# Sixteen batches of a scan, an FP4 network and linear attention on one core: every step's place in the engines' orders set anew

## The reference

```python
x = x + scan(layernorm(x))        # state-space scan, 16 states
x = x + ffn(layernorm(x))         # gate, up, down with FP4 blocks of 16
x = x + attention(layernorm(x))   # causal linear attention, 16 heads
x = x + ffn(layernorm(x))         # the same weights again

# scan
x_in = x @ w_in
dt_low, B, C = split(x_in @ w_x)                 # 64, 16, 16 columns
dt = softplus(dt_low @ w_dt + b_dt) * (DT_MAX - DT_MIN) + DT_MIN
A = -exp(A_log)
h = exp(dt * A) * h + sum_d(dt * A * B * u)      # step by step over 512 rows
y = sum_n(h * C) + Dp * u
# ffn: q() rounds blocks of 16 to FP4 with a scale of its own
y = q(silu(q(x) @ q(w_gate)) * (q(x) @ q(w_up))) @ q(w_down)
# attention: elu + 1 on q and k, sums over all rows so far
num = q_t @ sum(k v);  den = q_t @ sum(k);  y = (num / den) @ W_proj + b_proj
```

## Time and profile before

| | us |
|---|---|
| runs shown: lowest, median, highest of 3 | 2395.42, 2399.52, 3922.05 |
| profiled execution | 2388.81 |
| its span | 2387.1 |
| mean granted TensorE clock | 0.956 |

### The profile page before, as it was taken

The page is one execution under the profiler, slowest core; times in us unless marked ns, Lnnn a source line. Parts: engine busy times, 40 slices in busy tenths (PEclk is TensorE's granted clock), DMA queues, the critical chain, the costliest instruction groups (busy, mean ns, idle before and its releaser), DMA issues. The chain is left out here.

```text
span 2387.1 us, 40867 instructions
## 1 busy us (share of the span) xinstructions
PE 2074.3 (87%) x12844; PEld 1296.4 (54%) x12844; DVE 2055.3 (86%) x3876; ACT 1893.9 (79%) x3800; POOL 1210.0 (51%) x1804
## 2 busy tenths in 40 slices
PE   2448898998989899898989989898998989889887
PEld 1115556464655646465565646556564656646574
DVE  7988998979889897989989798998979899897734
ACT  5779887897978789797878979787897978867453
POOL 7114454545545454554546455454645555464744
PEclk8669899999999999999999999999999999999999
DMA  3542422323132232313223232322223132221000
GB/s 84 134 113 54 107 56 66 83 60 92 47 105 56 70 79 63 89 47 104 56 71 79 65 87 50 102 56 75 75 66 85 52 100 56 70 70 34 5 6 12
DMA packets 104452, 165.98 MB, mean 70 GB/s; under 512 B 15459, under 2 KB 34095, under 8 KB 104239
## 3 DMA queue, kind: packets, MB, share of 16 engines
q1 hardware_dynamic: 104238, 163.37, 25.7%
HBM read 146.55 MB, written 16.78 MB: 68 GB/s over the span
## 5 line engine op out<-in xcount | busy, mean ns | idle before, releaser
L1399 DVE TENSOR_TENSOR_SCAN scan_bufs<-scan_bufs,inp_bank 128x512 f32<-128x512 f32 x512 | 617.8, 1207 | 4.9 <-ACT scan_bufs L794 4.4
L1108 PE MATMUL bank<-w_gu,f_xqT 128*128 128x512 f32 x1024 | 496.6, 630 | 36.3 <-ACT f_xqT L857 35.1
L787 ACT ACTIVATE scan_bufs<-scan_bufs,a_rows 128x512 f32<-128x512 f32 x512 | 371.5, 725 | 54.8 <-DMA scan_bufs<-dt_copy 54.5
L1123 PE MATMUL bank<-w_dn,f_hqT 128*128 128x256 f32 x1536 | 357.9, 383 | 8.6 <-ACT f_hqT L857 8.6
L1108 PEld LDWEIGHTS bank<-w_gu,f_xqT 128*128 128x128 f32 x1024 | 201.1, 202 | 269.1 <-issue 265.0
L1409 DVE TENSOR_TENSOR scan_bufs<-scan_bufs,c_bank 128x512 f32<-128x512 f32 x512 | 343.1, 670 | 1.2
L794 ACT ACTIVATE scan_bufs<-scan_bufs 128x512 f32<-128x512 f32 x512 | 323.6, 632 | 3.9
L1123 PEld LDWEIGHTS bank<-w_dn,f_hqT 128*128 128x128 f32 x1536 | 284.3, 190 | 77.3 <-issue 26.0
L688 POOL TENSOR_TENSOR f_h<-f_h,f_h_scale 128x704 f32<-128x704 f32 x128 | 178.1, 1391 | 283.8 <-DVE f_h L1274 283.8
L710 POOL TENSOR_SCALAR_AFFINE_SELECT masked_scores<-masked_scores 128x512 f32<-128x512 f32 x256 | 168.8, 685 | 217.1 <-ACT masked_scores L857 216.8
L699 POOL TENSOR_TENSOR f_h<-f_h,f_h_lean 128x704 f32<-128x704 f32 x128 | 216.1, 1688 | 122.2 <-DVE f_h L1460 113.1
(11 more groups left out here) (196 smaller groups left out, 4408.3 us busy)
## 6 DMA issues: line engine op xcount, KB each, us to landing
scan_bufs<-dt_copy SPq DMA_DIRECT2D x512, 256.0 KB, 4.1
xp<-L_attn_a_x SPq DMA_DIRECT2D x16, 512.0 KB, 4.1
dt_copy<-dt SPq DMA_DIRECT2D x32, 256.0 KB, 2.8
out<-x SPq DMA_DIRECT2D x64, 128.0 KB, 3.5
w_attn<-L_attn_b_W_attn SPq DMA_DIRECT2D x1, 768.0 KB, 4.9
masked_scores<-L_ffn_w_gate SPq DMA_DIRECT2D x1, 704.0 KB
masked_scores<-L_ffn_w_up SPq DMA_DIRECT2D x1, 704.0 KB
f_h<-L_ffn_w_down SPq DMA_DIRECT2D x2, 352.0 KB, 11.1
```

The lines of the kernel that those rows point to most:

```text
L787: nc.scalar.activation(half, half, ACT.Exp, scale=a_rows[:, c, at:at + 1]).then_inc(root_ready, 1)
L1108: last = nc.tensor.matmul(to[:, :], f.xqT[:, k, :], w_gu[:, k, g, lo:hi], start=(k == 0), stop=(k == DH - 1))
L1123: last = nc.tensor.matmul(to[:, 0:D], f.hqT[:, k, :], w_dn[:, k, :], start=(k == 0), stop=(k == FK - 1))
L1399: nc.vector.tensor_tensor_scan(half, half, inp[:, :], 0.0, ALU.mult, ALU.add)\
```

## The change

All numbers that place steps are replaced. HEAD is written out step by step and its unit is one beat (`HEAD_BEAT` was 0.6), TIMES has new values, LAST_AT and LAST_SHIFT become GAPS and SHIFT. One wait is added: `inp` now names that ACT has copied `B` out of its bank. No instruction that computes is added or removed, but ACT loads its function table 65 times in place of 63, as `log` and `inv` of the two halves of batch 0 now alternate.

```diff
-HEAD_BEAT = 0.6
+HEAD_BEAT = 1.0
 HEAD = {
-    "dve": [(8.0, "P", 0, "stats"), (9.0, "P", 0, "aggr"), (10.0, "W", 0, "tables"),
+    "dve": [
+        (-132.873, "P", 0, "stats"), (-63.924, "P", 0, "aggr"), (-96.677, "W", 0, "tables"),
...
-LAST_AT = {"R1": (66, 3), "R2": (94.7, 4)}
-LAST_SHIFT = {
+GAPS = {(15, 'R2'): -3.0}
+SHIFT = {
+    15: {
...
 TIMES = {
-        ("Y", "finish"): -0.561, ("R1", "a_qkv"): 17.259, ("R2", "down"): 13.035, ("P", "stats"): 3.643,
+        ("Y", "finish"): -0.815, ("R1", "a_qkv"): 17.501, ("R2", "down"): 13.085, ("P", "stats"): 3.232,
...
 def beat_of(engine, part, step, t, b):
-    at = start_of(engine, part, step, t)
-    if b == NB - 1 and part in LAST_AT:
-        first, gap = LAST_AT[part]
-        at += first - PARTS_AT[part][0] + t * (gap - PARTS_AT[part][1])
-        at += LAST_SHIFT.get(engine, {}).get((part, step), 0.0)
+    at = start_of(engine, part, step, t) + t * GAPS.get((b, part), 0.0)
+    at += SHIFT.get(b, {}).get(engine, {}).get((part, step), 0.0)
     return round(BEATS * b + at, 6)
...
                     src, done = wait_filled(dve, "P", b, 0, "G")
+                    wait_drained(dve, "P", b, 0, "B")
```

More of the change, by code:

```diff
@@ L38 @@
 TURNS = PIECES + 4
-HEAD_BEAT = 0.6
-def pieces(step, first, gap, which):
-    return [(first + gap * n, "W", i, step) for n, i in enumerate(which)]
+HEAD_BEAT = 1.0
 HEAD = {
-    "sp": [(-40.0, "P", 0, "load"), (1.6, "P", 0, "keep0"), (8.6, "P", 0, "keep1")],
-    "dve": [(8.0, "P", 0, "stats"), (9.0, "P", 0, "aggr"), (10.0, "W", 0, "tables"),
[L50 to L64, removed]
[5 rows of a table removed]
[L70 to L75, removed]
@@ L76 @@
+    "sp": [
+        (89.322, "P", 0, "load"), (-65.789, "P", 0, "keep0"), (12.989, "P", 0, "keep1"),
+    ],
+    "dve": [
[17 rows of a table added]
+    ],
+    "pool": [
[6 rows of a table added]
+    ],
+    "act": [
[13 rows of a table added]
+    ],
[7 rows of a table added]
+    ],
 }
 PARTS_AT = {"P": (0, 0, 1), "M": (32, 1, 32), "D": (32, 2, 16), "G": (32, 4, 8), "S": (48.95, 16, 2), "Y": (65.0, 1, 2), "R1": (66, 3, 4), "R2": (95.7, 7, 4)}
-LAST_AT = {"R1": (66, 3), "R2": (94.7, 4)}
-LAST_SHIFT = {
[6 rows of a table removed]
-    },
-    "dve": {
[10 rows of a table removed]
-    },
-    "act": {
[7 rows of a table removed]
-    },
-    "pool": {
[5 rows of a table removed]
-    },
-    "sp": {
-        ("R2", "down"): 9.347,
+GAPS = {(15, 'R2'): -3.0}
@@ L123 @@
+SHIFT = {
[7 rows of a table added]
+        },
+        "dve": {
[10 rows of a table added]
+        },
+        "act": {
[7 rows of a table added]
+        },
+        "pool": {
[5 rows of a table added]
+        },
+        "sp": {
+            ("R2", "down"): -3.354,
+        },
     },
@@ L128 @@
     "sp": {
-        ("P", "load"): -24.91, ("P", "keep0"): 0.981, ("P", "keep1"): 5.167, ("D", "spread"): -29.206,
-        ("R2", "down"): -1.737,
+        ("P", "load"): -21.752, ("P", "keep0"): 4.226, ("P", "keep1"): 7.517, ("D", "spread"): -27.626,
+        ("R2", "down"): 0.583,
     },
     "pe": {
[7 rows of a table removed]
[7 rows of a table added]
     },
     "act": {
[14 rows of a table removed]
[14 rows of a table added]
     },
     "dve": {
[13 rows of a table removed]
[13 rows of a table added]
     },
     "pool": {
[5 rows of a table removed]
[5 rows of a table added]
     },
```

## The result

| | before | changed |
|---|---|---|
| median of 20 runs, us | 2394.16 | 2402.20 |
| range of the runs shown, us | 2390.44 to 3922.05 | 2398.60 to 2409.47 |
| profiled span, us | 2387.1 | 2397.0 |
| batch 0's `inp` at | 73.44 | 79.68 |
| batch 1's, batch 2's `inp` at | 146.74, 264.36 | 152.05, 265.65 |

The changed kernel is slower: ratio 1.0038, 95% interval 1.0031 to 1.0044. (One of before's runs, at 3922, was disturbed and is not in the ratio.) The 9.9 us between the two spans are laid out by the `inp` steps: +6.2 up to batch 0's, -0.9 from there to batch 1's, -4.0 to batch 2's, +10.7 over the thirteen periods behind it (0.8 each), -2.1 in the rest.

What follows compares the result with a forecast made beforehand. PE was taken to bound a period's second half, PE and DVE the first. 2388.8 + 9.5 (head) - 22 (steady part) - 3 (last batch) = 2373.3 profiled, plus 10.7 gives 2384 us; own range 2370 to 2396, wide 2343 to 2428.

Steps and rivals of the forecast that it cites:

- The steady part: Fourteen periods from batch 1's `inp` to batch 15's: -1.6 us each, -22 in all; bounds -4 and +2.2 a period.
- fall into a wait of DVE: Steady period: `soft1`, `sum1` and `dt1` on DVE land where it waits for ACT behind M29; priced at 0.
- PE's wait for `sp_pos`: Steady period: PE's 1.54 us bank wait goes, but two thirds come back on ACT; -0.5, between -1.5 and +1.
- that for `f_xqT`: Steady period: PE's 2.58 us wait for ACT's copy shortened by one decay (0.7); priced 0, between -0.7 and 0.
- that for the masked scores: Steady period: PE's 1.23 us wait for POOL shortened, as `a_s0` precedes `round_h`; -0.5, between -1.2 and 0.
- only three places that count: PE idles only for ACT's `f_xqT` copy (2.58 us), the `sp_pos` bank (1.54) and POOL's masked scores (1.23).
- The sign of being wrong that I had named: Period stays at 139 or grows, with PE idle before `turn_h`, which needs `abs_h`; or batch 0's `inp` before 76.
- Rival 2: Second half of a period: ACT's later `abs_h` and `abs_x` delay PE, +2.2 us a period, 2437 us; chance 0.20.
- The head: From the start to batch 1's `inp`: +9.5 us, bounds +3 and +14.
- The links: Head's five-part chain: late `aggr` and `norm`, results through bank 0, ACT's softplus work, `dt0` to first decay, late `B` copy.
- The two table loads: Head, ACT: two more loads of 1.28 us, 2.6 in all; with the skill's drain they would cost 5.3.
- The last batch: Behind batch 15's `inp`: a fifth of PE's idle 14.8 us gained, -3, between -6 and 0.

Runs made afterwards that it cites:

- experiment 13: Changed kernel with four long POOL products of a batch, those beside which DVE steps were lengthened, cut to 16 of 704 columns: 2354.5 us in one run.
- experiment 14: Control: changed kernel with four other long POOL products, beside which no DVE step was lengthened, cut to 16 of 704 columns: 2401.8 us in one run.
- experiment 11: Kernel before with all 24 long POOL products of a batch cut to 16 of 704 columns: 2351.0 us in one run.
- experiment 1: Changed kernel with DVE's `sum0` and `dt0` set back behind `a_sum` of R1's first tile: 2390.0 us, ratio 0.9986 to the kernel before.
- experiment 12: Changed kernel with all 24 long POOL products of a batch cut to 16 of 704 columns: 2318.0 us in one run.
- experiment 4: Kernel before with the new head's table, its unit and the added wait: 2402.3 us, ratio 1.0035.
- experiment 3: Changed kernel with the old head's table and its unit: 2393.4 us, ratio 1.0000 to the kernel before.
- experiment 9: Changed kernel with banks dealt as free from beat -1000 in place of 0: 2398.3 us, ratio 1.0026 to the kernel before.
- experiment 8: Changed kernel with `aggr`, `rstd`, `norm` and the first projections' copies early again in the head: 2405.3 us in one run.
- experiment 7: Changed kernel with ACT's copy of `B` back ahead of the first decay in the head: 2400.7 us in one run.

## Why the prediction was wrong

**The steady part, the step that failed.** I had -1.6 us a period and got +0.8. The terms were priced with the durations of the trace before, as if an instruction kept its length wherever it stands. It does not: four DVE instructions came to start while POOL multiplies, and cost 2.9 us a period (experiments 13, 14); a fifth, `soft0`, is held 1.1 us, at a price that no run gives. In the old order all of POOL's long products together held up no more than 1.5 (experiment 11). I had the means to see it: the earlier trace rows show a `lean_x` at 0.43 and the same step takes 1.10 at 1279.71 beside POOL, and `lean_h` takes 1.11 beside POOL and 0.88 elsewhere. I read such lines as spread. The Trainium skill, "GPSIMD Engine Reference", section "1. Specifications", says that POOL's interfaces to SBUF are shared with VectorE, with contention for DVE instructions that have two SBUF inputs or run in a 2-port mode. The trace agrees for the roundings and `soft0`, which have two SBUF inputs (0.89 to 2.25 us, 0.68 to 1.81), and for scans and reads, whose second input lies in PSUM and which were not held. `scale_x`, with one input, was held too (0.16 to 1.62 us); whether it ran in a 2-port mode no row shows.

The second loss was one I looked at and priced at nothing: softplus steps "fall into a wait of DVE". For `soft1`, `sum1` and `dt1` that was right. `sum0` and `dt0` had moved too, some 7 and 13 us earlier counted from `inp`, and I had not asked what stood behind them: `a_sum`, for whose bank PE waits. It cost 1.5 us a period (experiment 1), 0.95 by the wait itself and the rest where the G matmuls behind it ran slow.

Without the collisions the order is indeed a gain: with all long products cut in both kernels the new one has the shorter period by 2.4 us, the bank wait still in it (experiments 11 and 12). The single terms came in part: PE's wait for `sp_pos` is gone; that for `f_xqT` fell from 2.58 to 1.2 or 1.3 in the two periods with the G matmuls at the upper clock level, and to 0.6 only where they were at the lower one; that for the masked scores fell from 1.23 to 1.1 only, not by 0.5. So these terms had the right sign and were outweighed by what I had left out. PE also did not stand still at "only three places that count": the waits of the kernel before have a fourth of that size, 1.5 us ahead of a G step for DVE's read.

The sign of being wrong that I had named came: the period grew, and PE is idle before `turn_h`. But it waits there for POOL behind DVE's `round_h`, not for ACT's `abs_h`. One rival was neither named nor tested: from batch 3 on the new numbers hand 1179 of 1534 bank uses to another bank, and what that alone gives or costs in a period is open. Rival 2 (slower, ACT's steps pass through) had the sign by another mechanism: ACT's busy time rose by 0.5 us in a period (116.95 to 117.42 in the windows), and no wait of PE or DVE for the steps it names grew to what it needed.

**The head.** Forecast and measured: `norm` 26.8 and 25.7, the first softplus step 44.5 and 42.6, `dt0` 72.4 and 68.6, the first decay 78.9 and 75.2, `inp` 83.3 and 79.7; in the run with the slow clock (experiment 4) `dt0` came at 72.9, the decay at 79.1, `inp` at 83.6. The links were the right ones, but their sizes were too large by 1.9 us up to the softplus step and by another 1.9 from there to `dt0`. That experiment 4 meets the forecast is luck: it got there by slow matmuls, for which the sum had no term. At batch 1's `inp` I had +9.5; +5.3 was measured against before, 6.7 with nothing but the head exchanged in the changed kernel (experiment 3), 11.6 with it exchanged in the kernel before and the slow matmuls (experiment 4). What I had not foreseen is why everything fell to one bank (experiment 9), and that undoing `aggr` alone would bring nothing (experiment 8). The two table loads took 1.28 us each and the `log` began 0.01 us behind the load, which itself began 0.02 us behind the instruction ahead of it: there is no room for a drain of 1.38 us on either side.

**Between batch 1 and 2** the new TIMES gained 4.0 us, and I had no term for it: I took all fourteen periods as steady ones, though the first had 117.6 us, with only part of the work in it.

**The last batch.** -2.1 us behind batch 15's `inp`, forecast -3. That it came is not shown: the same last batch took 314.2 us here, 315.3 in experiment 3, 316.9 in experiments 7 and 9, against 316.3 and (experiment 4) 317.1 with the old numbers.

**The base and the range.** The median of three that I built on was 10.7 us above the profiled execution, that of twenty 5.4; the sum on the better base would be 2379 against 2394. The measured 2402 lies outside the forecast's own range (2370 to 2396) and inside the wide one (2343 to 2428). That the wide one held is luck, as it was made for other causes. And 2% is far from the least that can be told here: twenty runs of each kernel tell 0.4% from none.
